# Four feature chunks projected ahead of the steps instead of five, in a graph layer with a normalised 4096 x 4096 adjacency

## The reference

```python
h = maximum(layernorm(x), 0)                  # x: 4096 x 256
rowsum = adj.sum(axis=1)                      # adj: 4096 x 4096
d = where(rowsum > 0, rowsum ** -0.5, 0)
support = (d[:, None] * adj * d[None, :]) @ h
out = x + relu(support @ W + b)               # W: 256 x 256
```

## Time and profile before

| | before |
|---|---|
| median of 3 runs | 393.66 us (393.49 to 393.8) |
| the profiled execution | 393.01 us, of which span 391.2 us |
| PE busy | 383.5 us (98%) |
| DVE, ACT, POOL busy | 317.9, 288.7, 115.0 us |
| transfers | 151.86 MB, mean 388 GB/s |

### The profile page before, as it was taken

How to read it: one execution, slowest core, us unless ns; L and a number is a source line. 1 busy time by engine, 2 the same in 40 slices (tenths; PEclk the granted TensorE clock), 3 DMA queues, 4 the chain that set the end, 5 groups by cost and what they waited for, 6 DMA issues and landing times. The chain is left out here.

```text
span 391.2 us, 5139 instructions
## 1 busy us (share of the span) xinstructions
PE 383.5 (98%) x1754; PEld 319.9 (82%) x1754; DVE 317.9 (81%) x312; ACT 288.7 (74%) x286; POOL 115.0 (29%) x253
## 2 busy tenths in 40 slices
PE   8998999999999999999999999999999999999995
PEld 8886888888888888888888888888888888888884
DVE  6839966899686899958689995868899497889996
ACT  2889898788787878679878867978886793346533
POOL 2470335653121226114235811422520144000000
PEclk9999999999999999999999999999999999999999
DMA  7999999999999999999999999999999965997665
GB/s 296 427 421 426 426 424 427 425 429 428 422 423 424 427 427 429 420 426 424 424 428 426 428 419 428 425 425 427 428 426 429 404 229 220 394 372 255 214 169 207
DMA packets 24216, 151.86 MB, mean 388 GB/s; under 512 B 3328, under 2 KB 3328, under 8 KB 7552
## 3 DMA queue, kind: packets, MB, share of 16 engines
q1 hardware_dynamic: 24192, 151.55, 94.5%
HBM read 147.33 MB, written 4.22 MB: 387 GB/s over the span
## 5 line engine op out<-in xcount | busy, mean ns | idle before, releaser
L441 ACT ACTIVATE hi<-at,s 128x1024 fp32r<-128x1024 f32 x112 | 122.9, 1144 | 44.5 <-issue 32.5
L928 PE MATMUL moved<-hi,G 128*128 128x512 f32 x384 | 149.6, 390 | 1.5 <-DVE acc L729 1.5
L930 PE MATMUL moved<-hi,G 128*128 128x512 f32 x384 | 149.4, 389 | 0.0
L929 PE MATMUL moved<-lo,G 128*128 128x512 f32 x384 | 149.4, 389 | 0.0
L713 DVE SCALAR_TENSOR_TENSOR lo<-at,s,hi 128x1024 fp32r<-128x1024 f32 x112 | 140.8, 1278 | 9.1 <-ACT hi L441 9.1
L732 DVE TENSOR_TENSOR acc<-moved,acc 128x1024 f32<-128x1024 f32 x84 | 102.7, 1223 | 50.5 <-PE moved L930 50.5
L431 ACT ACTIVATE nat<-nat 128x2048 f32<-128x2048 f32 x64 | 122.1, 1908 | 7.8 <-DMA nat<-in_adj 7.8
L928 PEld LDWEIGHTS moved<-hi,G 128*128 128x128 f32 x384 | 72.1, 188 | 17.0 <-DVE acc L729 1.9
L930 PEld LDWEIGHTS moved<-hi,G 128*128 128x128 f32 x384 | 72.1, 188 | 15.0
L929 PEld LDWEIGHTS moved<-lo,G 128*128 128x128 f32 x384 | 72.1, 188 | 14.9
L601 POOL TENSOR_TENSOR row_sum<-part 128x1 f32<-128x1 f32 x32 | 17.9, 561 | 183.2 <-ACT nat L431 183.0
(11 more groups left out here) (75 smaller groups left out, 253.3 us busy)
## 6 DMA issues: line engine op xcount, KB each, us to landing
nat<-in_adj SPq DMA_DIRECT2D x64, 1024.0 KB, 13.8
at<-in_adj_t SPq DMA_DIRECT2D x64, 1024.0 KB, 12.4
acc<-in_x SPq DMA_DIRECT2D x4, 512.0 KB, 7.1
nat<-d_dram SPq DMA_DIRECT2D x2, 1024.0 KB, 5.8
nat<-in_x_t SPq DMA_DIRECT2D x4, 512.0 KB, 6.0
turned<-in_x_t SPq DMA_DIRECT2D x4, 512.0 KB, 6.9
out<-nat SPq DMA_DIRECT2D x4, 512.0 KB, 5.1
turned<-in_x SPq DMA_DIRECT2D x3, 512.0 KB, 14.7
```

What stands on the lines that cost most here:

```text
L441: nc.scalar.activation(hi[g % RING][:, 2 * c:2 * c + 2, :], at[g % LA][:, 2 * c:2 * c + 2, :], ACT.Copy, scale=s[:, j:j + 1]).then_inc(hi_ ...
L928: nc.tensor.matmul(into[:, f, :], big, hi[g % RING][:, t, :], start=begins, stop=False)
L929: nc.tensor.matmul(into[:, f, :], big, lo[g % RING][:, t, :], start=False, stop=False)
L930: mm = nc.tensor.matmul(into[:, f, :], small, hi[g % RING][:, t, :], start=False, stop=ends)
```

## The change

Chunk 4 goes from the front into the steps: `AHEAD` is 4, and `MADE_IN` becomes `{4: 4, 5: 6, 6: 9, 7: 11}`. Chunk 2 is turned and projected by halves, as chunk 1 was. VectorE adds up half row-blocks 1 and 3 (`sum_early`). GpSimd makes rstd of chunks 1 to 3 behind the scales of tiles 0 and 1. The orders of ScalarE and VectorE around step 0 are rewritten.

```diff
-AHEAD = 5
-MADE_IN = {5: 5, 6: 8, 7: 11}
+AHEAD = 4
+MADE_IN = {4: 4, 5: 6, 6: 9, 7: 11}
+BY_VECTOR = (1, 3)
-OFF_BY_GPSIMD = (3, 4)
-AT_ONCE = {0: 1, 1: 2}
+OFF_BY_GPSIMD = (3,)
+AT_ONCE = {0: 1, 1: 2, 2: 2}
...
         def wait_summed(eng, m):
-            eng.wait_ge(nat_summed, m + 1)
+            dve_part = len([e for e in BY_VECTOR if e <= m])
+            at_least(eng, nat_summed, m + 1 - dve_part)
+            at_least(eng, dve_summed, dve_part)
...
-            load_nat(EARLY - 1)
+            for m in range(AHEAD - 2, EARLY):
+                load_nat(m)
...
-            for t in range(BW):
-                take_part(0, t)
-            take_part(1, 0)
-            take_part(1, 2)
-            round_w()
-            for c in range(AHEAD - 2):
-
+            for c in range(OWN):
                 if c == 2:
-                    sum_nat(2)
-                round_raw(c)
-                if c < 2:
-                    sum_nat(c)
-                if c + 2 < FIRST_PART:
-                    take_turned(c + 2)
-                else:
-                    take_high(c + 2)
-                if c == 2:
-                    sum_nat(3)
-
-            round_slot(0)
+                    round_raw(0)
+                for t in range(0, BW, AT_ONCE[c]):
+                    take_part(c, t)
+                    if (c, t) == (2, 0):
+                        round_w()
+            sum_nat(0)
+            round_raw(1)
+            take_turned(3)
+            sum_nat(2)
+
+            round_tile(0, 0)
+
+            round_raw(AHEAD - 2)
+            round_tile(0, 1)
             round_slot(1)
-            round_raw(AHEAD - 2)
             round_raw(AHEAD - 1)
...
             scale_of(0)
-            rstd_of(1)
-            rstd_of(2)
             scale_of(1)
+            for c in range(1, AHEAD):
+                rstd_of(c)
...
+            def sum_early(m):
+                dve.wait_ge(nat_landed[m % LN], DMA * (m // LN + 1))
+                nc.vector.reduce_sum(part[:, m // 2, m % 2:m % 2 + 1], nat[m % LN][:, :],
+                                     axis=mybir.AxisListType.X).then_inc(dve_summed, 1)
...
-            for n in range(4):
-                subtract(n // 2, n % 2)
+            take_stats(3)
+            rest_of_raw(0)
+            sum_early(1)
+            rest_of_raw(1)
+            rest_of_w()
+            sum_early(3)
+            subtract(0, 0)
             rest_of_raw(AHEAD - 2)
-            piece = 4
+            subtract(0, 1)
+            subtract(1, 0)
+            piece = 3
...
-                        if (g, p) == (2, 0):
+                        if (g, p) == (2, 1):
                             rest_of_raw(AHEAD - 1)
-                            continue
-                        for n in range(piece, 2 * g + p + 5):
+                        upto = 2 * g + p + (4 if g < 3 else 5)
+                        for n in range(piece, upto):
...
-            for c, n in ((1, 3), (2, 2), (3, 1)):
-                if n:
-                    project(c, range(n))
-                turn(c + 1)
-                project(c, range(n, BW))
-            project_parts(4)
+            project(1, range(2))
+            turn_part(2, 0)
+            project(1, range(2, 3))
+            turn_part(2, 2)
+            project(1, range(3, 4))
+
+            project(2, range(2))
+            turn(3)
+            project(2, range(2, BW))
+            project(3)
```

More of the change, by code:

```diff
@@ L266, in build @@
         nat_summed = sem("nat_summed")
+        dve_summed = sem("dve_summed")
         s_ready = sem("s_ready")
@@ L463, in take_part @@
                 last = t + AT_ONCE[c] == BW
+                at_least(act, hW_done, c - 1)
                 if last:
@@ L474, in round_w @@
                 nc.scalar.copy(w_hi[:, :, :], w_sb[:, :, :]).then_inc(w_hi_made, 1)
-            def take_high(c):
-                act.wait_ge(h_turned, c + 1)
-                nc.scalar.activation(hT_part(c, 0), pair_of(("turn", c))[:, :, :], ACT.Relu).then_inc(hT_hi_made, 1)
             def rectify_h(c):
@@ L631, in _ @@
                 scale_of(j)
-                if OWN <= j - 2 < AHEAD:
-                    rstd_of(j - 2)
             pool.wait_ge(b_landed, DMA)
@@ L670, in rest_of_w @@
                                         op=ALU.subtract).then_inc(w_parts_ready, 1)
[L672 to L676, removed]
             def shift(c):
@@ L797, in _ @@
                         gather(k, 2 * q + p)
-                        if (g, p) == (2, 0):
+                        if (g, p) == (2, 1):
                             rest_of_raw(AHEAD - 1)
-                            continue
-                        for n in range(piece, 2 * g + p + 5):
+                        upto = 2 * g + p + (4 if g < 3 else 5)
+                        for n in range(piece, upto):
                             subtract(n // 2, n % 2)
-                        piece = 2 * g + p + 5
+                        piece = upto
                 elif NARROW[k]:
@@ L851, in turn_part @@
             def turn_part(c, t):
-                if c == 1 and t > 0:
-                    pe.wait_ge(hT_ready, 1)
+                if c == 0:
+                    at_least(pe, part_hT_ready, part_before(c, t) - 2)
+                elif t == 0:
+                    pe.wait_ge(part_hT_ready, part_before(c, t) - 1)
                 else:
-                    at_least(pe, part_hT_ready, part_before(c, t) - (2 if c == 0 else 1))
+                    pe.wait_ge(hT_ready, c)
                 for tile in range(t, t + AT_ONCE[c]):
```

## The result

The changed kernel is slower: its runs lie between 395.73 and 399.22 us where those of before lie between 393.35 and 393.80 (medians 398.12 and 393.54). The ratio is 1.0102, with a 95% interval of 1.0082 to 1.0122, or 4.0 us. (One execution at a granted clock of 0.56 is left out.) On a second chip the ratio was 1.0074 (1.0060 to 1.0087), 3.0 us. The forecast was +1.6 us with a range up to 396.5. The profiled execution took 396.82 us, so it is one of the quicker ones; its span is 395.0, against 391.2 before, 3.8 us more; the clock was 1.00 in every stretch looked at, 0.998 as a mean.

What follows compares the result with a forecast made beforehand. TensorE, always busy from 35.58 us, was taken as the bound, with transfers just behind. A remaining lead of 1.2 us against 2.8 us of projection gave +1.6 us, 395.3 us on the median; range 393.4 to 396.5.

Steps and rivals of the forecast that it cites:

- The front: Before the steps: slot 0 starts at 24.5 us instead of 28.30, and TensorE is 5.7 us ahead at slot 1.
- The lead handed back: At slots 2, 3, 7 and 12 TensorE's lead of 5.7 us falls to 1.2 us.
- Slots 2, 3 and 7: Three places where TensorE's lead falls: to 4.0 us, then 2.7 us, then 1.55 us.
- slot 12: Chunk 4's second load adds 1.2 us to the queue; the gather ends at 91.5, TensorE wants 91.15; lead 1.2 us.
- the lead left at slot 7: After a wait for the gather in slot 6, TensorE is still 1.55 us ahead.
- The projection: Chunk 4's 24 matmuls move from the front and return in step 5, costing 2.8 us there.
- the way of chunks 5 to 7, which cost TensorE no wait: Chunk 4's statistics, shift, rounding and remainder in the steps cost TensorE nothing; the added 0.75 MiB stays inside the margin.
- The rival of a queue running dry: At 24 us, chunk 4's load waits and holds back later transfers: +2.8 us, 396.5; chance 0.15 with the failed front.
- The weighing of the shared port: VectorE and GpSimd taking turns might delay slot 1 from 29.9 to 30.5 us; slot 2 starts at 37.05 either way.
- the slow row: Profile row where tile 1's product d took 0.79 us while VectorE was subtracting, against 0.19 for tile 0.

Runs made afterwards that it cites:

- Experiment 1: The changed kernel with the loads of chunks 6 and 7 issued three slots later in SP's order; 395.42 us, ratio 1.0041.
- Experiment 3: The changed kernel with all four late chunk loads issued three slots later in SP's order; 394.90 us, ratio 1.0036.
- Experiment 5: The changed kernel itself timed again beside the kernel before; 396.81 us, ratio 1.0074.
- experiment 2: The kernel before with SP made to wait at slots 20 and 28 for VectorE's second piece of that slot; 394.53 us, ratio 1.0014.
- experiment 9: The kernel before with the remainder of chunk 3's product moved on VectorE behind the gather of panel 3; 393.62 us, ratio 0.9996.
- experiment 10: The kernel before with chunk 3's remainder behind the gather of panel 3 and VectorE's pieces of slots 3 to 11 one place later; 393.55 us, ratio 0.9995.

## Why the prediction was wrong

- **The front** came as worked out: slot 0 at 24.92 (24.5 forecast), 5 us ahead at the gathers of panels 2 and 3 (5.7). VectorE's sum of 2048 numbers took 2.28 us (2.2).

```profile
15.48 2.28 DVE L666 TENSOR_REDUCE part<-nat 128x1 f32<-128x2048 f32 x1
```

- **The lead handed back.** Slots 2, 3 and 7 were right as places; at slot 12 nothing was lost, because the lead was already below its margin. What was mis-sized is the lead left at slot 7: 0.4 us, where I had 1.55 there and 1.2 at the end. The transfers of slots 2 and 3 took this long from issue to landing (compare):

```profile
L381 SPq DMA_DIRECT2D at<-in_adj_t x2: 441/446/450, 21.6 to 22.1; - x2
DMA to landing us min/median/max: 12.5/13.5/14.5
```

Slot 2 landed at 21.6 + 12.5 = 34.1 instead of 33.4, and slot 7 at 61.0 instead of 60.35. And ScalarE was not free when slot 7 landed: it was summing a half block, and its first piece started 0.5 us after the landing.

```profile
61.49 2.18 ACT L447 ACTIVATE hi<-at,s 128x1024 fp32r<-128x1024 f32 x2
```

I had that start at the landing, 60.35. It came 1.14 us later, and 1.55 - 1.14 = 0.41 is the lead that was measured. A little over half of the shortfall is the landing, the rest ScalarE's order. Experiments 1 and 3 bear the sum out: ScalarE started slot 7 at 61.15 and 60.86, and the lead behind it was 0.7 and 1.0. This is 0.8 us of the error in the span (1.2 forecast, 0.4 measured).
- **The projection** was right: 2.8 us.
- **The step that failed** is the sentence that the later course of chunk 4 stays inside the margin, "the way of chunks 5 to 7, which cost TensorE no wait". I counted the bytes that the change adds and not the waits that it moves. The load of chunk c waits for the low part of chunk c-2; the new `MADE_IN` puts the load of chunk 6 two slots behind chunk 4's low part and that of chunk 7 two behind chunk 5's, while SP runs four slots ahead. SP waits 14.7 us twice, with every transfer of the adjacency behind it. I put the cost at nothing; it was 1.4 us in the trace and 1.3 to 2.4 in the medians. Experiment 1 takes just that away and the time falls to 395.42. Experiment 5 repeats the loss.
- **That experiment 1 meets the +1.6 us of the forecast** is in part luck. Trace against trace it is 2.5 us slower than before (spans 393.7 and 391.2), since the lead is 0.4 and not 1.2. But the first profile of before was a quick execution. In experiment 2, which is the same kernel up to slot 20, slot 2 landed 1.0 us later and TensorE was 1.0 behind from there on. The median of before seems to hold such a loss, and in the comparison of medians it stands in for the lead that was missing.
- **The rival of a queue running dry** was named, at 24 us and for chunk 4's load. The shortage came with the waits from 122 and 169 us, for chunks 6 and 7. Chunk 4's load waited too, 12.9 us for TensorE, but was issued at 20.25, before it did harm.
- **The weighing of the shared port** would change nothing, as said: d of tile 1 took 0.82 us beside VectorE's remainder, as in the slow row, slot 1 followed slot 0 without a wait, and the gather of panel 4 set slot 2.

What stays open: the first result lies 1 us higher over before than experiment 5 does, and its slower executions (398.12 to 399.22) have no trace; the two traced ones of this kernel show 1.3 to 1.4 us of late loss. Why the same wait cost 0.5 us in experiment 2 is argued there, not shown. The wait, the 0.75 MiB and the later projection meet in one margin, and no run separates the last two.

## What to carry to other kernels

When one queue issues all transfers in order, a step's move has to be checked against every wait in that queue: take the slot in which the queue comes to the wait, add how far it runs ahead, and compare it with the slot in which the awaited work is done. A busy engine can hide such a wait: here TensorE lost its time some 120 us after the end of the first one. So look at the waits of the engine that reads the landed data. And when a transfer is worked out to land earlier, check that the engine that takes it up is free by then. A lead won in the front is only worth what the narrowest later margin lets through, so widen that first.

## What the runs showed of the hardware

SP issued nothing for 14.7 us twice, and the rate of transfers in these pauses was 415 and 426 GB/s, all but what it was with SP issuing (425 to 428): the last slot issued ahead of the first pause landed 17.8 us after its issue, so that much work was outstanding. The dip came at the end of the pauses and behind them (374 GB/s from 141 to 151 us, 325 from 183 to 192). The landing of the same early transfer, slot 2, moved by 1.2 us (33.4 to 34.6) between the profile of before and those of experiments 2, 9 and 10, whose transfers are the same up to it, and that was as much as several of the effects studied here.
